# A two-layer transformer block: projections that leave tokens on the partitions, and gates as rows applied by VectorE

## The reference, cut to what matters

```python
mod = (_silu(c) @ wmod).reshape(8, 6, 1, -1)        # per batch: six rows of 128
sa, ca, ga, sb, cb, gb = mod[:, 0], ..., mod[:, 5]
ga = (2 * (ga >= 0) - 1) * jnp.maximum(jnp.abs(ga), 0.25)   # gb likewise
x = x + ga * attention(_layernorm(x) * (1 + ca) + sa)
x = x + gb * experts(_layernorm(x) * (1 + cb) + sb)
```

## Time and profile before

| | |
|---|---|
| median of 3 runs | 773.23 us (772.94 to 774.85) |
| the profiled execution, its own time | 775.72 us |
| its span in the profile | 773.8 us |
| mean granted TensorE clock | 0.989 of full |
| busy: PE, DVE, ACT, POOL | 744.0, 555.0, 381.5, 186.7 us |
| weight loads of PE (PEld) | 563.1 us |

### The profile page before, as it was taken

The page is one execution under the profiler, slowest core; times in us unless marked ns, Lnnn a source line. Parts: engine busy times, 40 slices in busy tenths (PEclk is TensorE's granted clock), DMA queues, the critical chain, the costliest instruction groups (busy, mean ns, idle before and its releaser), DMA issues.

```text
span 773.8 us, 16795 instructions
## 1 busy us (share of the span) xinstructions
PE 744.0 (96%) x6559; PEld 563.1 (73%) x6559; DVE 555.0 (72%) x1639; ACT 381.5 (49%) x1059; POOL 186.7 (24%) x233
## 2 busy tenths in 40 slices
PE   7799998999999999999999999999989898999996
PEld 5566756775787578657866876678477777999996
DVE  4887874869676876778677867797949663265986
ACT  3755555356535654564456535633641444544422
POOL 0234221153116301530253035205200421000000
PEclk9999999999999999999999999999999998999999
DMA  8930020402040204020301121021204304000000
GB/s 236 397 93 7 28 56 2 109 1 56 3 109 1 57 2 110 2 55 22 91 19 38 46 67 43 16 68 43 56 2 110 110 17 95 1 1 1 14 22 22
DMA packets 55702, 43.07 MB, mean 56 GB/s; under 512 B 37900, under 2 KB 48804, under 8 KB 54216
## 3 DMA queue, kind: packets, MB, share of 16 engines
q1 hardware_dynamic: 55624, 42.01, 20.4%
HBM read 32.42 MB, written 9.58 MB: 54 GB/s over the span
## 4 chain that ended last, share of the span: by engine, by line
PE 90%; DVE 5%; DMA 2%; issue 1%; POOL 1%; ACT 0%; SPq 0%; DVEq 0%; ACTq 0%
PE ps L1734 15%; PE ps L1813 14%; PE ps L1865 8%; PE ps L2023 6%; PE ps L2001 6%; PE ps L1970 4%; PE ps L1720 4%; PE ps L1742 4%; PE ps L1833 3%; PE ps L1766 3%; PE ps L1755 3%; PE ps L1884 2%; PE ps L1683 2%; PE ps L1656 2%; PE ps L1672 2%; PE ps L1927 2%
## 5 line engine op out<-in xcount | busy, mean ns | idle before, releaser
L1734 PE MATMUL ps<-veF,hB 128*128 128x512 f32 x256 | 121.6, 606 | 0.0
L1289 DVE COPY_PREDICATED shared<-ghot,ps 128x512 f32<-128x512 int32 x128 | 88.3, 727 | 3.1 <-PE ps L1734 0.2
L828 ACT ACTIVATE sc<-sc,nmax 128x128 f32<-128x128 f32 (+1 forms) x128 | 57.2, 447 | 58.7 <-DVE nmax L1275 58.7
L1734 PEld LDWEIGHTS ps<-veF,hB 128*128 128x128 f32 x256 | 45.2, 189 | 49.4 <-issue 39.9
L630 POOL TENSOR_TENSOR sc<-sc,rg 128x384 f32<-128x384 f32 x64 | 51.7, 829 | 69.9 <-DVE rg L1262 69.9
L687 POOL TENSOR_TENSOR ve<-mv,eps 128x2 f32<-128x2 f32 x24 | 8.6, 359 | 241.9 <-DVE mv L1175 241.9
L1865 PE MATMUL ps<-hC,early 128*64 128x128 f32 x1024 | 63.6, 280 | 2.7 <-ACT hC L746 1.6
L1813 PE MATMUL ps<-early_masks,oeF 128*128 128x256 f32 x256 | 62.9, 385 | 1.2 <-issue 1.2
L1865 PEld LDWEIGHTS ps<-hC,early 128*64 128x64 f32 x1024 | 57.3, 140 | 8.3 <-issue 4.6
L1813 PE MATMUL ps<-wide,oeF 128*128 128x256 f32 x256 | 62.5, 386 | 0.0
L2001 PE MATMUL ps<-hE,veF 128*128 128x256 f32 x256 | 58.7, 382 | 0.0
(11 more groups left out here) (252 smaller groups left out, 1535.3 us busy)
## 6 DMA issues: line engine op xcount, KB each, us to landing
chosen<-hot_scratch SPq DMA_DIRECT2D x16, 512.0 KB, 5.8
v_scratch<-shared SPq DMA_DIRECT2D x16, 512.0 KB, 5.2
vg<-v_scratch SPq DMA_DIRECT2D x16, 512.0 KB, 5.6
veF<-in_L_ffn_value_experts SPq DMA_DIRECT2D x1, 2048.0 KB, 9.3
oeF<-in_L_ffn_output_experts SPq DMA_DIRECT2D x1, 2048.0 KB, 14.0
early<-in_L_attn_w_qkv SPq DMA_DIRECT2D x1, 1536.0 KB, 14.5
shared<-bias_scratch SPq DMA_DIRECT2D x2, 512.0 KB, 5.5
veF<-in_L_ffn_W SPq DMA_DIRECT2D x1, 1024.0 KB, 5.3
```

Source lines behind the costliest of these rows:

```text
L828: act.activation(v, v, ACT.Exp, bias=nmax[:, h % RING, t:t + 1], scale=-1.0, accum_out=denB[:, h * T + t:h * T + t + 1]).then_inc(s_("f_e" ...
L1289: dve.copy_predicated(val[:, t, :].rearrange("p (h k) -> p h k", h=HF), ghot[:, t * HF:(t + 1) * HF, e].bitcast(I32).unsqueeze(2) .broadca ...
L1734: pe.matmul(ps[:, vbank(j), :], tok(hB, t), veF[:, :].rearrange("p (h e k) -> p e h k", h=HF, e=EF)[:, e, :, :], start=True, stop=True).th ...
```

## The change

**Projections.** The tokens become the loaded operand and the weights are streamed: each matmul of 256 columns becomes two of 128, one per tile of tokens, and the result has tokens on the partitions. `yT`, its 24 ACT copies and the 24 pairs of transposes back go. The products now write two banks, 5 and 7, so they wait for all four score quarters (`c_sc` at `b * 4` in place of `(b - 1) * 4 + 2`). For `wo1` the copies to `o1T` must now leave the tokens in order: their innermost run is 4 elements that lie 32 elements apart.

**Gates.** They are rows of 128 along the free axis. DVE clips them in [8 x 256] tiles (four operations at ROWS0 in the opening, five at MODDED), SP writes them to memory, and `load_row` reads them back to all partitions: four rows of 128 for each batch, in four slots of `gate_rows`. `add_to_x` now has two DVE operations, a multiplication out of PSUM by the row and the addition to `x`. POOL adds the row gate x `b_out` to `x` at MODULATE of the ffn (`bo_added`). The modulation matmuls become four and one wide one; the four small gate operations on [128 x 16] go, with `gsign`, `gabs`, `boga`.

**New waits on PE.** Where a bank was free once `yT` was copied, it is now free after DVE's multiplication (`y_used`): ahead of the gates matmul of `values(b)` for b > 0 and ahead of group 0 of `back1(6)`.

**Order.** In `values` ADD, NORM and MODULATE of the ffn stand at "start", 1 and 3 (before: PROJECT at "start", ADD at 1, NORM 3, MODULATE 5). In the experts the six steps of the last batch stand some three places earlier, and `FIRST_SLOT` is 18. In the opening the sum of the `Wo` fold is issued before the second half of batch 1's scores, the exponentials of batch 1's heads 2 and 3 stand behind the copy `oTA` of batch 0, and four of the early transposes moved from the products into `values(0)` (`TURNED_45`, with ACT in place of DVE for two of the copies).

```diff
@@ the order
-            in_values = {"start": (PROJECT,), 1: (ADD,), 3: (NORM,), 5: (MODULATE,)}
+            in_values = {"start": (ADD,), 1: (NORM,), 3: (MODULATE,)}
-            in_experts = {(0, 25): (PROJECT,), (0, 28): (ADD,), (0, 29): (NORM,), (1, 5): (MODULATE,), (1, 9): (LOGITS,),
-                          (1, 15): (PROBS,)}
+            in_experts = {(0, 25): (PROJECT, ADD), (0, 26): (NORM,), (1, 2): (MODULATE,), (1, 6): (LOGITS,),
+                          (1, 12): (PROBS,)}
@@ out_o1: where the copies to o1T write
-            w = 2 * TURNED * GT
-            v = o1T[hp * DH:(hp + 1) * DH, :, c * P + g * w:c * P + (g + 1) * w]
-            return v.rearrange("p h (n t) -> p h n t", t=GT)
+            w = 2 * TURNED
+            v = o1T[hp * DH:(hp + 1) * DH, :, c * P:(c + 1) * P].rearrange("p h (t n) -> p h n t", t=GT)
+            return v[:, :, g * w:(g + 1) * w, :]
@@ PE, woT0
-                    for m in range(2):
-                        mm = pe.matmul(ps[:, 0, 0:N], woT0[:, m, :], oTA[:, m, :], start=(m == 0), stop=(m == 1))
+                    for t in range(T):
+                        for m in range(2):
+                            mm = pe.matmul(ps[:, 0, t * P:(t + 1) * P], oTA[:, m, t * P:(t + 1) * P], woT0[:, m, :],
+                                           start=(m == 0), stop=(m == 1))
-                if n == ADD:
-                    back(b, "a_ys", "a_yt")
@@ PE, products
-                    pe.wait_ge(s_("c_sc"), (b - 1) * QUARTERS + 2)
+                    pe.wait_ge(s_("c_sc"), b * QUARTERS)
-                        mm = pe.matmul(ps[:, 5, 0:N], oeF[:, c // 4, (2 * c + j) % 8, :], masked(c)[:, j, :],
-                                       start=(c == 0 and j == 0), stop=(c == 15 and j == 1))
+                        for t in range(T):
+                            mm = pe.matmul(ps[:, 5 + 2 * t, 0:P], masked(c)[:, j, t * P:(t + 1) * P],
+                                           oeF[:, c // 4, (2 * c + j) % 8, :], start=(c == 0 and j == 0),
+                                           stop=(c == 15 and j == 1))
@@ PE, values, ahead of the gates matmul
+                            pe.wait_ge(s_("y_used"), added_products(b - 1) + 1)
@@ PE, wo1
-                    for j in range(H1 // 2):
-                        mm = pe.matmul(ps[:, 0, 0:N], wo1[:, j, :], o1T[:, j, :], start=(j == 0), stop=(j == 7))
+                    for t in range(T):
+                        for j in range(H1 // 2):
+                            mm = pe.matmul(ps[:, 0, t * P:(t + 1) * P], o1T[:, j, t * P:(t + 1) * P], wo1[:, j, :],
+                                           start=(j == 0), stop=(j == 7))
@@ DVE
-            def add_to_x(b, k, what):
-                dve.wait_ge(s_(what), b + 1)
-                dve.tensor_tensor(xb(b), xb(b), ps[:, 0, 0:N].rearrange("p (t d) -> p t d", t=T),
-                                  ALU.add).then_inc(s_("x_done"), 1)
-                wait_apart(dve, (s_("x_done"), k + 1))
+            def add_to_x(b, k, y, row):
+                dve.wait_ge(s_("row%d" % row), b * 16 + 16)
+                dve.tensor_tensor(gated_y[:, :, :], y,
+                                  gate_rows[:, row, :].unsqueeze(1).broadcast_to([P, T, D]), ALU.mult).then_inc(s_("y_used"), 1)
+                dve.wait_ge(s_("y_used"), k + 1)
+                dve.tensor_tensor(xb(b), xb(b), gated_y[:, :, :], ALU.add).then_inc(s_("x_done"), 1)
+                dve.wait_ge(s_("x_done"), k + 1)
@@ SP
+            def load_row(i, b):
+                sp.dma_start(gate_rows[:, i, :], gate_dram[b, i, :].partition_broadcast(P)).then_inc(s_("row%d" % i), 16)
@@ POOL, MODULATE of after_products
+                    pool.wait_ge(s_("n_xn"), k * 2 + TILES + T)
+                    pool.wait_ge(s_("row3"), b * 16 + 16)
+                    pool.tensor_tensor(x[:, b * T:(b + 1) * T, :], x[:, b * T:(b + 1) * T, :],
+                                       gate_rows[:, 3, :].unsqueeze(1).broadcast_to([P, T, D]),
+                                       ALU.add).then_inc(s_("bo_added"), 1)
@@ the opening
+            opening(0, 0, SUMO)
+            attn0(1, 0, S1)
             opening(0, 0, FOLDO)
             attn0(1, 0, N0)
-            attn0(1, 0, S1)
             attn0(0, 0, V1)
             attn0(0, 0, OUT)
+            attn0(1, 0, EXP2)
             after_attn0(0, 0, PROJECT)
+            attn0(1, 0, EXP3)
             attn0(1, 0, T0)
+            after_attn0(0, 0, ADD)
             attn0(1, 0, N1)
-            after_attn0(0, 0, ADD)
```

More of the change, by code:

```diff
@@ L55 @@
 EXACT = 11
[L56 removed]
+SLOTS, SLOTS_A_STEP, FIRST_SLOT = 32, 5, 18
 PROB_BITS = 30
@@ L228, in adaln_kernel @@
                   "route": ["bits", "bitsf", "rm"], "experts": ["w1", "w2"],
-                  "bias": ["rb", "oneh"], "small": ["bsel"], "first": ["x01"]}
+                  "bias": ["rb", "oneh"], "first": ["x01"]}
         group_of = {n: g for g, names in groups.items() for n in names}
@@ L411, in in_order @@
             opening(0, 0, FOLDV)
+            opening(0, 0, ROWS0)
             for n in (S0, S1, VP):
@@ L438, in in_order @@
             values(0, 1, beside((after_attn0, 1, 1, in_values_first), (attn0, 1, 0, {"queries": (V1, OUT)}),
-                                (opening, 0, 0, {"start": (NORMED,), 2: (TURNED_NEXT,), "turns": (NORMED_LAST,)}),
+                                (opening, 0, 0, {"start": (NORMED, NORMED_LAST), 2: (TURNED_NEXT,), "turns": (TURNED_45,), "end": (HELD_45,)}),
                                 (attn0, 2, 0, {4: (TAKE,)})))
@@ L546, in _ @@
             spread(0)
-            sp.wait_ge(s_("g8"), 1)
-            sp.dma_start(gate_dram, g8[:, 0, :]).then_inc(s_("bias_out"), 16)
-            sp.wait_ge(s_("bias_out"), 32)
-            sp.dma_start(gate1[:, :, :], gate_dram.partition_broadcast(P)).then_inc(s_("gate1"), 16)
-            with sp.Fori(0, B - 1) as b:
-                spread(b + 1)
-                relay(b)
+            sp.wait_ge(s_("y_used"), added_attn0(0) + 1)
+            load_row(0, 1)
+            sp.wait_ge(s_("y_used"), added_attn0(1) + 1)
+            load_row(0, 2)
+            sp.wait_ge(s_("rows1"), 1)
+            sp.dma_start(gate_dram[:, 2:5, :], g8[:, 2:5, :]).then_inc(s_("bias_out"), 16)
+            sp.wait_ge(s_("bias_out"), 48)
+            load_row(2, 0)
+            load_row(3, 0)
+            for b in range(B - 1):
+                spread(b + 1)
+                sp.wait_ge(s_("y_used"), added_products(b) + 1)
+                load_row(1, b + 1)
+                if b + 3 < B:
+                    sp.wait_ge(s_("y_used"), added_attn0(b + 2) + 1)
+                    load_row(0, b + 3)
+                relay(b)
+                sp.wait_ge(s_("bo_added"), b + 1)
+                load_row(3, b + 1)
+                if b > 0:
+                    sp.wait_ge(s_("y_used"), added_attn1(b - 1) + 1)
+                    load_row(2, b)
             sp.wait_ge(s_("f_yp"), B * 16)
@@ L695, in after_attn1 @@
                     pool.tensor_copy(hE[:, bass.ds(b * N, N)], hR[:, :]).then_inc(s_("h_kept"), 1)
-            beside = in_order(attn0, values, nothing, front1, back1, products, nothing, opening, last_softmax, after, after,
+            beside = in_order(attn0, values, nothing, front1, back1, products, nothing, opening, last_softmax, after, after_products,
                               after_front1, after_attn1)
@@ L1549, in modulations @@
                 bank, at = mod_at(l)
-                for k in range(6):
-                    mm = pe.matmul(ps[:, bank, at + k * B:at + (k + 1) * B], wm[l][:, k * D:(k + 1) * D],
-                                   csT[:, l, :], start=True, stop=True)
-                mm.then_inc(s_("mod_p"), 1)
+                for k in (0, 1, 3, 4):
+                    pe.matmul(ps[:, bank, at + k * B:at + (k + 1) * B], wm[l][:, k * D:(k + 1) * D], csT[:, l, :],
+                              start=True, stop=True)
+                pe.matmul(ps[0:B, 4 * l, N * (1 - l):N * (1 - l) + 2 * D], csT[:, l, :],
+                          wm[l].rearrange("p (k d) -> p k d", d=D)[:, 2::3, :], start=True,
+                          stop=True).then_inc(s_("mod_p"), 1)
             def fold(i):
@@ L1586, in opening @@
                     pe.wait_ge(s_("a_sc"), 12)
-                    pe.matmul(ps[0:B, 4, 0:D], csT[:, 1, :], wm[1][:, 5 * D:6 * D], start=True, stop=True)
                     modulations(1)
@@ L1606, in tok @@
                 return h[:, t * P:(t + 1) * P]
-            def back(b, ready, done):
-                pe.wait_ge(s_(ready), b + 1)
-                for t in range(T):
-                    mm = pe.transpose(ps[:, 0, t * P:(t + 1) * P], yT[:, t * P:(t + 1) * P], ident[:, :])
-                mm.then_inc(s_(done), 1)
             def attn0(b, k, n):
@@ L1818, in after_products @@
             def after_products(b, k, n):
-                if n == ADD:
-                    back(b, "f_ys", "f_yt")
                 if n == MODULATE:
@@ L1946, in back1 @@
```

(2 more changed lines are left out.)

128 lines of the change are left out of this document (69 added, 59 removed).

## The result

The changed kernel takes 798.94 us (median of 4, 797.62 to 800.2) against 773.09 for the kernel before: ratio 1.0331, 95% interval 1.0306 to 1.0356, +25.9 us. Its profiled execution took 797.62 with a span of 795.7. The prediction had the sign, but only +5 us, and its range ended at 783.

What follows compares the result with a forecast made beforehand. PE was taken to bound the kernel, DVE second. Opening -2.8, first rounds +0.4, rounds 1 to 4 +2.6, round 5 +2.3, front1(6) +1.0, values(7) -0.3, end +2.1: +5.3, said as +5, so 778 us; 8-in-10 range 771.5 to 783.

Steps and rivals of the forecast that it cites:

- the sign: Whole kernel: the change makes it slower, by +5 us.
- each is issued a stage ahead of its use, so I count nothing: Gate-row loads, four small transfers a batch: 0 us; if one were late, DVE would wait at its add.
- the order of ADD, NORM and MODULATE in values and experts moves by some places and keeps its distance to PE's use: nothing: DVE's moved steps in values and experts: the new order costs 0 us.
- The `o1T` copies: Scattered single-element writes: +0.24 us for each of ACT's 64 copies; DVE's taken as 0, bounds 0 and +0.24.
- front1 step: In front1, longer copies and the multiplication delay DVE's copies of the values past slack 0.56: PE's L1625 starts 0.5 later.
- For a round the forecast: Rounds 1 to 4: front1, products and `wo1`, less transposes, plus the wait ADDS passes on: +0.65 us each.
- The `c_sc` wait: Products(6) and (7) wait for four score quarters instead of two: +1.2 us each; hidden in rounds 0 to 5.
- the rival "slower still": PE's clock falls behind waits ahead of products(6) and (7), +1.9 us each, or DVE's copies pay too: 781.5; chance 0.17.
- More instructions: Projections on PE: two 128-column matmuls replace one of 256, +0.0073 us each, 672 times: +4.9 us.
- The multiplication: DVE's extra operation per add: +0.41 us, 24 times; in values and products it lies in DVE's free quarter.
- The opening: Copy `oTA` ahead of four exponentials, -3.0 us; row operations +0.6, transposes moved into values(0) -0.4: -2.8; first projection near 32.
- the 778: Forecast time of the changed kernel against the median of the runs before, 773.23 us.

Runs made afterwards that it cites:

- experiment 1: Changed kernel with SP issuing the load of batch 1's first gate row ahead of the transfers of batch 0's chosen experts: 790.77 us.
- experiments 5 and 6: Changed kernel: 5 keeps only the multiplication at the start of values, later steps moved back, 792.82 us; 6 moves POOL's four multiplications first, DVE's order kept, 792.77 us.
- experiment 12: The kernel with the four mends, without gates: DVE adds y straight from PSUM, no multiplication; 768.78 us, -3.2 against the four mends alone.
- experiment 8: Kernel before with one edit: the products wait for four score quarters in place of two; 774.87 us, +1.9.
- experiment 10: Changed kernel with the four mends together: early gate-row load, o1T copies with loops turned, addition in values cut in two, both product tiles in one bank; 772.02 us.

## Why the prediction was wrong

**The step that failed most** is the sentence on the gate rows: "each is issued a stage ahead of its use, so I count nothing". It looked at the DMA engines' 17% and not at what stands ahead of the load in SP's queue. Batch 1's row is the one whose slot comes free late and whose use is early, and its load stood behind a transfer that waits for `hotT`. Measured: 8.2 us (experiment 1). The consequence that the prediction named (DVE waits "with the next masks and copies behind it") is what happened.

**The second** is "the order of ADD, NORM and MODULATE in values and experts moves by some places and keeps its distance to PE's use: nothing". Measured: 6.1 and 6.2 us (experiments 5 and 6), by way of POOL, whose four multiplications slid onto DVE's argmax. The prediction had looked at POOL's deadlines and not at who runs beside it.

**The `o1T` copies**: mechanism right, size wrong. ACT's +0.24 was +0.265; for DVE I took 0 of the bounds 0 and 0.24, and it was 0.209. What hangs on them came to 9.8 us, where the forecast holds about half of that. Its front1 step was wrong in the detail: the wait for the copies of the values stays at 0.5 us without the longer copies and goes with the multiplication (experiment 12), so it is the multiplication that uses up the slack of 0.56, and the longer copies show up as waits before the first queries and before L1746. For a round the forecast was +0.65; it became +2.3, of which 0.8 hang on the copies, 0.8 on POOL and 0.7 on the multiplication.

**The `c_sc` wait**: +1.2 twice, as forecast (1.19 measured in experiment 8). In the trace of the changed kernel the clock fell at the first of them, the mechanism of the rival "slower still"; undoing the waits gave 3.3 in the changed kernel, and adding them cost the kernel before 1.9.

**More instructions**: right. `wo1` of batch 0 in the chain of the changed kernel:

```profile
227.96 3.13 PE ps L2025 x28
```

3.13 / 28 = 0.112 us each. **The multiplication**: 3.2 us, counted mostly as free time of DVE. A quarter of free time is no cover where PE waits for the end of a DVE sequence: in products PE waits 0.34 us for `xn`, in four rounds, for which the forecast had nothing. **The opening**: the first projection starts at 31.86 us (forecast near 32), and values(0) 3.5 earlier against 2.8 forecast. **POOL's addition of the bias** shows no wait of PE behind it.

That the sign came out right is not luck: the copies and the `c_sc` wait were both named. But without the two causes that it put at nothing the changed kernel would be near 784.6 us (an estimate, 798.94 - 8.2 - 6.1; no run has this), still 6 to 7 above the 778, and above the range. So the terms that it did count were too small as well, the copies above all.

The four mends together return 26.9 of the +25.9 us, so the rest of the change (its opening, its missing transposes, its multiplication and added instructions) is worth -1.3 by experiment 10, with an interval that includes 0. What the missing transposes and the added instructions are worth by themselves no run shows.

## What to carry to other kernels

A load that depends on nothing expensive is still as late as whatever its queue waits for: for each new transfer write down the wait that stands ahead of it in its own queue, above all for the first use after the opening. When a step is moved on one engine, list the steps of every engine that hang on it, and look at what they will then run beside; DVE operations with two operands in on-chip memory next to POOL's large ones are the pair to look for. If a copy must change the layout, turn its loops so that the scattered side is the read from PSUM: here it was free, and the scattered write took 49% (DVE) and 70% (ACT) longer. Where single runs scatter by some microseconds, compare a stage that repeats: here the rounds told 0.8 us apart.

## What the runs showed of the hardware

- A copy of 64 x 256 out of PSUM that writes single float32 values 128 bytes apart takes ACT 643 ns instead of 378, and DVE 633 instead of 424. The same copy with 8 neighbours written and PSUM read 256 bytes apart takes 377 and 423.
- A DVE operation of 128 x 128 with two operands in on-chip memory takes 0.29 us alone and 0.69 to 1.01 beside POOL's multiplications of 128 x 512 (about 1.04 us each, which they keep), and ends some 0.15 us behind the end of one of them; a reduction with one operand keeps its 0.29.
- The clock fell to its lower level, 1.2 GHz, behind the opening's wait of 3.0 us in two of four traces; it cost 1.6 us there. At products(6) it fell with a wait of 2.07 us and stayed with one of 2.38, so the length of the wait alone did not decide it.
- A load of 64 KB took 4.1 us from issue to landing at 42.5 us, with the DMA engines full, and 6.3 us right behind transfers of 1 MB.
